# Two batches of a first layer open at once: other PSUM banks, other homes in SBUF, constants in two loads, new lists

## The chip, the cores and the metric

One NeuronCore of one Trainium2 chip runs the whole program. Its engines are called here as in the profile: PE (TensorE), DVE (VectorE), ACT (ScalarE), POOL (GpSimd) and SP (SyncE, which only issues transfers). The metric is the device time of one execution in microseconds (us), lower is better.

## The reference

Two layers follow each other for 8 batches of 256 tokens with 256 features. The first is a graph attention with 16 heads and two directions, in which each of the 256 tokens looks at the first 20 only. The second is a transformer block with adaptive norm, rotary embedding, full attention over 256 tokens (16 heads of 16) and a gated feed-forward part of width 1024.

```python
# first layer
row_zero = exp_v.sum(-1) == 0
q_exp = jnp.where(row_zero[..., None], 0.0, q[:, None, :])
self_feat = jnp.concatenate([exp_v, q_exp], axis=-1) @ W_self.T + b_self
for d in range(2):
    A = (adj_f if d == 0 else jnp.swapaxes(adj_f, 1, 2))[:, :, :20, :]
    cond, vb = A.sum(-1), A @ w_bias + b_bias
    # qh from self_feat, kh from its first 20 rows
    aff = jnp.where(mask, qh_kh / sqrt(dh), NEG) + vb      # mask: cond > 0
    output = output + out_projection(softmax(aff) @ kv)
x = exp_v + relu(output)
# second layer
nx = ada_rmsnorm(x, time_emb, ...);  q, k = rope(nx @ wq + bq), rope(nx @ wk + bk)
x = x + softmax(q k^T / sqrt(16)) v @ wo + bo
x = x + (gelu(nz @ w_gate) * (nz @ w_up)) @ w_down         # nz = ada_rmsnorm(x, ...)
```

## The kernel before

**Stages.** Each engine works through a list of steps written out by hand, `step(n)(b)` for part n of batch b, in that order and without skipping; semaphores join the engines. Lists of neighbouring batches are interleaved: the first layer of batch b + 2 stands beside the second layer of batch b. All big products are made of three float32r products of high and low halves (`product`, L2109), so that each operand is split by a copy on ACT (`...h`, `whigh`) and a subtraction on POOL or DVE (`...l`, `low` L597, `wlow` L592 on POOL and L1496 on DVE).

**First layer of a batch, front.** DVE sums the rows of x (`rowsum`, L1532), POOL marks zero rows (`nonzero`), SP stores that mask to memory and reads it back broadcast (`nz_store` L278, `nz_load` L283), POOL makes of it and of the condition column the start of the self features (`nzq`, L616). PE adds the self product (`selfm`), DVE joins them (`selfc`, L1538 and L1539), PE makes small key and value products (`small` L2179, `kT`), DVE spreads them (`kev`, `vb`, `kb`), PE makes `q0` and the affinity (`affm`, L2212). DVE counts the adjacency (`adjm`, L1522 to L1526), POOL makes mask and bias of it (`mask`).

**Back.** DVE multiplies by the mask (`am`, L1569), POOL adds the bias (`aadd`, L641) and subtracts the maximum (`asub`, L649), ACT takes the exponential, POOL normalises (`aprob`, L662), PE transposes the probabilities (`pTt`, L2228; copies `pTa` on ACT, `pTc` on DVE), PE multiplies with the values (`y`, L2240), DVE adds (`yadd`, L1598), PE transposes (`x1T`, L2152), DVE makes x1 (`x1add`, L1604).

**PSUM and SBUF.** Front and back of this layer share PSUM banks 3 and 4: `BANK = {"c": 0, "self": 3, "k0": 4, "v0": 3, "q0": (3, 4), "aff": 3, "pT": (4, 3), "y": 4, "x1": 3, ...}`. They share the buffer `l0` as well (q0T, kblk and kk of the front, pT and yT of the back), `self32` and `vblk`. So `selfm(0)` of batch b waits for `x1_ok` of batch b - 1, `nzq` and `small` for its `y_ok`. Banks 0 and 1 serve the condition products at the start (`cond_1`, `cond_2`) and then the scores.

**Second layer.** `nxT`, `qk`, `v`, the rotation (`rot` on DVE L1625, `radd` on POOL L690), `qkT`, `qkadd` (DVE, L1641 and L1642), `qklow` (POOL, L698), out to memory and back in stacked form (`high_out`, `low_out`, `q_stack`, `k_stack` on SP), then 16 score products `s` (L2302) with 16 maxima `mx` on DVE (L1650), their transpose `nmT` (L2311), a row copied by `nrows`, 16 products `st` (L2326) with 16 exponentials `exph` on ACT (L1047), `pv`, `oT`, `aT`, `wo`, then gate, up and down products.

**Loads at the start.** SP loads x, weights in pieces of 256 KB into eight slots (a piece waits for the `wlow` of the one before it in its slot) and constants in seven loads: `get_consts`, `get_wb`, the condition column (in `cond`), `get_vec`, `get_angles`, `get_rope`, `get_bo`. The condition table `tab` is made by DVE in `table` out of `cond_2`.

Of the kernel before, what the change touches and what calls it, by code (L numbers as in the profile page):

```python
# [9 lines left out]
ALU = mybir.AluOpType  # L10
# [15 lines left out]
KC = D // P  # L26
# [8 lines left out]
BEHIND = 2  # L35

# [8 lines left out]
K_ID, K_M8, K_M4, K_ONES, K_BK, K_ALL = 0, 128, 136, 140, 156, 284  # L45
# [19 lines left out]
def build(nc, x, xT, adj, condT, wall, wsmall, wcond, cols, rows_in, tabs, consts_in, out):  # L65
    ctx = ExitStack()
    with ctx:
# [3 lines left out]
        def sig(name, per=1):  # L71
# [42 lines left out]
        pT = l0[:, :].rearrange("p (d g s) -> p d g s", d=2, g=4)  # L114
        yT = l0[:, 0:512].rearrange("p (k s) -> p k s", k=KC)
# [34 lines left out]

        wcq, wc1, wc2 = vv[:].rearrange("p c n -> p (c n)")[:, 0:512], t1[:].rearrange("p c n -> p (c n)"), ya[:, :]
# [62 lines left out]
        BANK = {"c": 0, "self": 3, "k0": 4, "v0": 3, "q0": (3, 4), "aff": 3, "pT": (4, 3), "y": 4, "x1": 3,  # L214
# [27 lines left out]
        def _(sp):  # L242
# [117 lines left out]
            get_wb()  # L360
            load_x(1)
            nz_store(0)
            weights("self", 0)()
            cond()
            load_adj(0)
            nz_load(0)
            nz_store(1)
            get_vec()
            get_wsk()
            get_wsv()  # L370
            weights("q0", 1)()
# [2850 lines left out]
```

## Time and profile before

| what | us |
|---|---|
| median of 3 runs | 514.03 |
| lowest, highest | 509.83, 514.95 |
| the profiled execution | 512.82 |
| its span, first to last instruction | 511.0 |
| mean granted clock of TensorE | 0.960 of full |

The span is read from the trace of one execution; the runs are timed from outside. Busy times are sums over an engine's instructions, and the chain is followed back from the last instruction to whatever released each.

### The profile page before, as it was taken

The numbers are of one execution on the slowest core, as the hardware profiler recorded it, in microseconds if no ns is written. First come the engines' busy times: TensorE is split into PE (matmuls) and PEld (weight loads), VectorE is DVE, ScalarE is ACT, GpSimd is POOL, SyncE is SP. The second block draws the span as 40 slices with busy tenths as digits, with TensorE's granted clock in tenths as the row PEclk, the third lists the DMA queues.
The fourth block names the chain that finished last, engine by engine and source line by source line (L and its number), as shares of the span: only waits on it lengthen the run. The fifth ranks groups of instructions, "written<-read, shape, count | busy, mean of one in ns | idle before, by whom it ended". The sixth has DMA issues, their size and how long they took to land.

```text
span 511.0 us, 9893 instructions
## 1 busy us (share of the span) xinstructions
PE 450.1 (88%) x3728; PEld 391.5 (77%) x3728; DVE 321.6 (63%) x529; ACT 245.0 (48%) x472; POOL 270.3 (53%) x266
## 2 busy tenths in 40 slices
PE   0776766878899999989999998999899979999997
PEld 0674655757588789878979897889788957897896
DVE  1757666898689547936995597478834870840421
ACT  1144412434722884177436843675466328347431
POOL 4555588597745655654554583546831371132232
PEclk9985787999889999999999998999999999999999
DMA  6920264614320430053014401540032003210000
GB/s 177 339 112 3 96 109 158 182 32 155 106 52 3 127 104 22 22 175 101 22 58 106 135 2 44 106 149 0 4 119 89 3 18 129 63 45 2 21 22 22
DMA packets 35231, 41.30 MB, mean 81 GB/s; under 512 B 5872, under 2 KB 27888, under 8 KB 35056
## 3 DMA queue, kind: packets, MB, share of 16 engines
q1 hardware_dynamic: 35184, 40.67, 27.3%
q8 instruction: 30, 0.49, 0.4%
q14 instruction: 17, 0.14, 0.1%
HBM read 29.90 MB, written 10.49 MB: 79 GB/s over the span
## 4 chain that ended last, share of the span: by engine, by line
PE 67%; DVE 12%; POOL 9%; issue 5%; DMA 4%; ACT 2%; SPq 1%; DVEq 0%; POOLq 0%; ACTq 0%
PE ps L2109 33%; PE ps L2326 7%; PE ps L2341 6%; PE ps L2302 5%; PE ps L2152 4%; PE ps L2228 3%; PE ps L2212 3%; PE ps L2240 3%; PE ps L2179 2%; DVE nm L1650 2%; POOL aff L641 2%; POOL prob L662 2%; DMA vec<-cols 1%; PE ps L2353 1%; DVE aff L1569 1%
## 5 line engine op out<-in xcount | busy, mean ns | idle before, releaser
L1650 DVE TENSOR_REDUCE nm<-ps 128x2 f32<-128x512 f32 x128 | 83.9, 683 | 26.3 <-PE ps L2302 25.8
L2109 PE MATMUL ps<-splz,wh 128*128 128x256 f32 x512 | 96.3, 286 | 3.0 <-DVE ya L1642 1.8
L1047 ACT ACTIVATE ex<-ps 128x512 f32<-128x512 f32 x128 | 70.0, 598 | 35.4 <-PE ps L2326 33.7
L2109 PEld LDWEIGHTS ps<-splz,wh 128*128 128x128 f32 x512 | 79.3, 191 | 5.5 <-issue 4.7
L597 POOL TENSOR_TENSOR hs<-g,hs 128x512 fp32r<-128x512 f32 x32 | 42.0, 1316 | 72.3 <-ACT hs L1091 72.3
L2109 PE MATMUL ps<-splz,wl 128*128 128x256 f32 x256 | 72.3, 282 | 0.0
L2302 PE MATMUL ps<-kst,qst 96*128 96x256 f32 x256 | 51.6, 305 | 4.9 <-DVE nm L1650 4.0
L2109 PE MATMUL ps<-wh,hs 128*128 128x256 f32 x256 | 52.8, 286 | 0.7 <-POOL hs L597 0.7
L2326 PE MATMUL ps<-qst,kst 100*128 100x256 f32 x256 | 49.2, 303 | 2.7 <-DMA qst<-ex 2.5
L1694 DVE TENSOR_TENSOR g<-ps,g 128x512 f32<-128x512 f32 x32 | 22.0, 687 | 46.4 <-PE ps L2109 41.0
L2109 PEld LDWEIGHTS ps<-splz,wl 128*128 128x128 f32 x256 | 48.8, 191 | 0.0
L2326 PEld LDWEIGHTS ps<-qst,kst 100*128 100x128 f32 x256 | 36.1, 189 | 15.9 <-ACT ex L1047 10.5
L2302 PEld LDWEIGHTS ps<-kst,qst 96*128 96x128 f32 x256 | 38.1, 192 | 12.5 <-DVE nm L1650 9.4
L2109 PEld LDWEIGHTS ps<-wh,hs 128*128 128x128 f32 x256 | 42.5, 191 | 1.0 <-POOL hs L597 0.9
L2109 PE MATMUL ps<-splx,wh 128*128 128x256 f32 x192 | 39.1, 302 | 3.1 <-DVE res L1604 2.3
L641 POOL TENSOR_TENSOR aff<-aff,off 128x640 f32<-128x640 f32 x16 | 26.6, 1663 | 23.3 <-DVE aff L1569 23.3
L2109 PE MATMUL ps<-wh,sply 128*128 128x512 f32 (+1 forms) x128 | 37.5, 357 | 0.1
L2109 PE MATMUL ps<-wl,hs 128*128 128x256 f32 x128 | 36.2, 283 | 0.0
L1081 ACT ACTIVATE g<-ps 128x512 f32<-128x512 f32 x32 | 19.1, 597 | 35.1 <-PE ps L2109 34.5
L2109 PEld LDWEIGHTS ps<-splx,wh 128*128 128x128 f32 x192 | 32.0, 205 | 4.8 <-DVE res L1604 3.1
L2341 PE MATMUL ps<-ex,vv 128*32 128x256 f32 x512 | 35.1, 393 | 0.2 <-ACT ex L1047 0.2
L597 POOL TENSOR_TENSOR splz<-ya,splz 128x512 fp32r<-128x512 f32 x16 | 20.5, 1283 | 26.8 <-DVE ya L1674 21.3
(131 smaller groups left out, 997.1 us busy)
## 6 DMA issues: line engine op xcount, KB each, us to landing
qk_d<-ya SPq DMA_DIRECT2D x32, 256.0 KB, 3.9
qst<-qk_d SPq DMA_DIRECT2D x48, 128.0 KB, 2.5
kst<-qk_d SPq DMA_DIRECT2D x96, 64.0 KB, 2.4
ex<-wall SPq DMA_DIRECT2D x15, 256.0 KB, 6.8
aff<-adj SPq DMA_DIRECT2D x8, 440.0 KB, 3.9
res<-x SPq DMA_DIRECT2D x8, 256.0 KB, 2.7
xTs<-xT SPq DMA_DIRECT2D x8, 256.0 KB, 3.6
result<-res SPq DMA_DIRECT2D x8, 256.0 KB, 2.0
```

The lines of the kernel that those rows point to most:

```text
L597: pool.tensor_tensor(into, whole, high.bitcast(FP32), ALU.subtract).then_inc(signal.sem, 1)
L641: pool.tensor_tensor(aff[:, c], aff[:, c], off[:, :, c, :].unsqueeze(2).broadcast_to([P, 2, H, M]), ALU.add).then_inc(aa_ok.sem, 1)
L1047: act.activation(ex[:, h % EXR], ps[:, h % 2].rearrange("p (c s) -> p c s", c=TC), ACT.Exp, scale=SCALE).then_inc(ex_ok.sem, 1)
L1081: act.activation(g32[:, j % 2], ps[:, BANK["g"]].rearrange("p (k s) -> p k s", k=2), ACT.Gelu).then_inc(gelu_ok.sem, 1)
L1650: dve.tensor_reduce(nm[:, :, h % 2, h // 2], ps[:, h % 2].rearrange("p (c s) -> p c s", c=TC), AX.X, ALU.max, negate=True).then_inc(mx_ok. ...
L1694: dve.tensor_tensor(g, ps[:, BANK["u"]].rearrange("p (k s) -> p k s", k=2), g, ALU.mult).then_inc(hm_ok.sem, 1)
L2109: ins = pe.matmul(dst, lhs(a, k), rhs(c, k), start=first_ and n == 0 and m == 0, stop=last_ and n == len(ks) - 1 and m == 2, **kw)
L2152: ins = pe.transpose(dst[:, i * S + j * P:i * S + (j + 1) * P], src(i, j), ident)
L2212: ins = pe.matmul(ps[:, 3 + d, k * 8 * M:(k + 1) * 8 * M], q0T[:, d, k, c * P:(c + 1) * P], kblk[:, 2 * d + k].rearrange("p h m -> p (h m) ...
L2302: ins = pe.matmul(ps[:, bk, c * S:(c + 1) * S], qst[0:96, h // 2, c * P:(c + 1) * P], kst[0:96, h, :], start=True, stop=True)
L2326: ins = pe.matmul(ps[:, bk, c * S:(c + 1) * S], kst[0:100, h, c * P:(c + 1) * P], qst[0:100, h // 2, :], start=True, stop=True)
L2341: ins = pe.matmul(ps[32 * j:32 * j + 32, 2, (g % 2) * S:(g % 2 + 1) * S], vv[:, c, h * VW:h * VW + 32], ex[:, h % EXR, c, :], start=c == 0 ...
```

## The change

- PSUM: for batches 0 and 1 (`OPEN = 2`) the back of the first layer uses banks 0 and 1 instead of 4 and 3.
- SBUF: for these two, pT and yT lie in `ya` instead of `l0`; self features and value blocks of batch 1 lie in `g32`.
- Waits: `selfm(0)` of batches 1 and 2 waits for `am_ok` of the batch before instead of `x1_ok`; `nzq`, `small` and `vb` of batches 1 and 2 don't wait for the back of the batch before (batch 2 for that of batch 0). New waits: `pTt` of batch 0 on the first half of the table, of batch 1 on `x1_ok` of batch 0; `nzq(1)` on the rotated bias; the first `gelu` on `y_ok` of batch 1; `qkadd` of batch 0 and `s(0)`, `s(1)` of batch 0 on `x1_ps` or `x1_ok` of batch 1.
- Loads: column constants, condition column and label row come inside `consts` (now 348 columns), rope and bo in one load `late`; angles stay alone. Four loads fewer.
- All five lists are new, over the whole program.

The core of the diff, in this order: banks and homes, the wait of `selfm`, that of `pTt`, that of `qkadd` for batch 0:

```diff
-        BANK = {"c": 0, "self": 3, "k0": 4, "v0": 3, "q0": (3, 4), "aff": 3, "pT": (4, 3), "y": 4, "x1": 3,
+        BANK = {"c": 0, "self": 3, "k0": 4, "v0": 3, "q0": (3, 4), "aff": 3,
...
+        early = ya[:, :]
+        spare = g32[:].rearrange("p j i s -> p (j i s)")
+        selves = [self32[:], spare[:, 0:KC * S].rearrange("p (k s) -> p k s", k=KC)]
+        vblks = [vblk[:], spare[:, KC * S:KC * S + 512].rearrange("p (d g n) -> p d g n", d=2, g=4)]
+        def pT_of(b):
+            return (early if b < OPEN else l0[:, :]).rearrange("p (d g s) -> p d g s", d=2, g=4)
+        def back(b, n):
+            return (0, 1)[n] if b < OPEN else (3, 4)[n]
...
 -                        before(pe, x1_ok, b - 1)
+                        if b <= OPEN:
+                            before(pe, am_ok, b - 1)
+                        else:
+                            pe.wait_ge(x1_ok.sem, x1_ok.at(b - 1))
...
 -                    if n < 2:
+                    if n < 2 and b == 0:
+                        pe.wait_ge(tab_ok.sem, tab_ok.at(0, 4))
+                    elif n < 2 and b < OPEN:
+                        pe.wait_ge(x1_ok.sem, x1_ok.at(b - 1))
+                    elif n < 2:
                         pe.wait_ge(am_ok.sem, am_ok.at(b))
...
 -                        dve.wait_ge(c2_ps.sem, c2_ps.at(0))
+                        dve.wait_ge(x1_ps.sem, x1_ps.at(OPEN - 1))
```

The lists up to the first score product, before and after (k(0) for step k of batch 0, several parts together):

```
PE before:  cond_q selfm(0) small(0) kT(0) q0(0) affm0(0) cond_1 affm1(0) cond_2 pTt(0) y(0) x1T(0)
            selfm(1) small(1) nxT(0) kT(1) q0(1) affm(1) qk0,v0,qk1,v1(0) pTt(1) qkT(0) y(1) x1T(1)
            selfm(2) nxT(1) small(2) q0,kT(2) s(0)
PE after:   cond_q selfm(0) small(0) kT(0) q0(0) affm0(0) cond_1 affm1(0) selfm(1) cond_2 small1(1)
            pTt0,1(0) small0(1) kT(1) pTt2,3(0) q0(1) y(0) x1T(0) affm(1) nxT(0) qk0(0) pTt0,1(1) qk1(0)
            pTt2,3(1) selfm0(2) y(1) selfm1(2) x1T(1) qkT(0) v(0) small(2) kT(2) q0(2) nxT(1) affm0(2) s(0)
DVE before: ... am0 amax0 am1 ones0 amax1 asums0 asums1(0) table pTc(0) ones1 wlow-v yadd(0) wlow-qk0
            x1add(0) rowsum(2) selfc kev vb kb adjm(1) nxc(0) am0(1) wlow-qk1 am1(1) wlow-u0 amax(1)
            rot0(0) asums(1) rot1(0) pTc1(1) rowsum(3) pTc3(1) qkadd(0) yadd x1add(1) adjm selfc(2) ...
DVE after:  ... am0 amax0 am1(0) rowsum(2) amax1 asums0(0) selfc(1) table asums1 pTc1(0) kev vb kb(1)
            pTc3(0) ones1 adjm(1) yadd x1add(0) am0(1) wlow-v am1 amax0(1) nxc(0) amax1(1) wlow-qk0,qk1
            asums(1) wlow-u0 rowsum(3) rot0(0) pTc1,3(1) rot1(0) wlow-u1 yadd(1) selfc(2) qkadd(0)
            x1add(1) kev vb kb adjm(2) nxc(1) wlow-u2 am0(2) mx0(0) ...
POOL after: nonzero(0) fills xl(0) nzq(0) zeros0 vfill selfl(0) nonzero(1) mask(0) xl(1) aadd0 asub0
            aadd1(0) nzq(1) asub1 aprob(0) selfl(1) wlow-g0,g1,g2 nonzero(2) wlow-g3 mask(1) wlow-d0
            pow1(0) aadd0,1 asub0(1) nxl(0) asub1 aprob0(1) xl(2) aprob1(1) radd0(0) nzq(2) nonzero(3)
            radd1(0) zeros1 selfl(2) qklow(0) pow1(1) ...
SP after:   x(0) consts adj(0) w-self angles xT(0) nz_store(0) wcond-q w-q0 nz_load(0) wsv wsk w-q0b x(1)
            late xT(1) w-g2 wc1 w-qk0 nz_store(1) wc2 nz_load(1) x(2) w-v w-g0 w-g1 w-qk1 adj(1) w-g3
            xT(2) w-d0 x(3) w-d1 nz_store(2) w-u0 w-u2 w-u1 xT(3) nz_load(2) w-d2 w-d3 adj(2) high_out ...
```

## Rows read from the trace of the kernel before

**Rows 1.** The page: busy us of each engine; shares of the chain.

```profile
PE 450.1 (88%) x3728; PEld 391.5 (77%) x3728; DVE 321.6 (63%) x529; ACT 245.0 (48%) x472; POOL 270.3 (53%) x266
...
PE 67%; DVE 12%; POOL 9%; issue 5%; DMA 4%; ACT 2%; SPq 1%; DVEq 0%; POOLq 0%; ACTq 0%
```

**Rows 2.** Busy time by stretch: us, engines' busy us, clock, DMA share, GB/s.

```profile
0.00:94.60 94.60, 58.37 (x396) 49.79 (x397) 57.91 (x94) 29.93 (x61) 58.65 (x63) 0.84 0.50 145
94.60:118.10 23.50, 18.90 (x130) 15.60 (x129) 21.51 (x36) 8.30 (x17) 18.07 (x17) 1.00 0.30 78
...
160.00:400.00 240.00, 233.16 (x2057) 206.93 (x2057) 162.73 (x268) 137.06 (x256) 131.90 (x128) 0.99 0.26 74
```

**Rows 3.** The chain in order of time, to 140 us: start us, us, what.

```profile
4.23 4.42 DMA nz_d<-nz
...
17.04 1.12 POOL self L616 x2
...
41.69 1.29 POOL prob L662
...
50.77 0.70 DVE res L1604
...
64.90 0.84 DVE aff L1569
...
84.42 1.05 POOL ya L698
...
94.75 0.47 PE ps L2302 x4
```

**Rows 4.** DMA issues up to 60 us: count, KB each, median us to landing.

```profile
ex<-wall SPq DMA_DIRECT2D x10, 256.0 KB, 8.4
...
ya<-wcond SPq DMA_DIRECT2D x1, 1024.0 KB, 10.6
...
nzb<-nz_d SPq DMA_DIRECT2D x2, 128.0 KB, 7.7
...
const_sb<-consts SPq DMA_DIRECT2D x1, 142.0 KB, 3.7
...
vec<-cols SPq DMA_DIRECT2D x1, 18.0 KB, 7.3
```

**Rows 5.** DVE in order of time: start us, us, operation.

```profile
41.26 1.74 DVE L1513 TENSOR_SCALAR tab<-tab,vec 128x8 f32<-128x8 f32 x4
...
59.35 1.06 DVE L1522 TENSOR_REDUCE aff<-aff 128x80 f32<-128x880 int32 x1
```

**Rows 6.** PE in order of time: start us, us, operation, idle before.

```profile
32.80 4.76 PE L2144 MATMUL ps<-hT,ya 128*128 128x8 f32 x32 [1.07 <-ACT hT L952]
...
45.88 3.41 PE L2240 MATMUL ps<-l,vblk 128*64 128x256 f32 x16 [0.83 <-issue]
...
78.93 1.94 PE L2228 MATMUL ps<-const_sb,prob 128*128 128x128 f32 x8 [1.56 <-POOL prob L662]
80.66 1.92 PE L2152 MATMUL ps<-const_sb,t 128*128 128x128 f32 x8
...
111.25 1.06 PE L2228 MATMUL ps<-const_sb,prob 128*128 128x128 f32 x8
...
113.16 1.95 PE L2240 MATMUL ps<-l,vblk 128*64 128x256 f32 x16 [0.26 <-issue]
```

**Rows 7.** POOL in order of time.

```profile
33.50 2.52 POOL L641 TENSOR_TENSOR aff<-aff,off 128x640 f32<-128x640 f32 x1
...
65.99 1.99 POOL L641 TENSOR_TENSOR aff<-aff,off 128x640 f32<-128x640 f32 x1
...
99.88 1.54 POOL L641 TENSOR_TENSOR aff<-aff,off 128x640 f32<-128x640 f32 x1 [3.77 <-DVE aff L1569]
```

**Rows 8.** SP's queue in order of time.

```profile
86.12 2.42 SPq L308 DMA_DIRECT2D qst<-qk_d  x3
```

**Rows 9.** Busy time from 40 to 50 us, columns as in rows 2.

```profile
40.00:50.00 10.00, 6.89 (x32) 4.63 (x30) 7.81 (x19) 3.82 (x8) 4.67 (x3) 0.56 0.00 0
```

More of the change, by code:

```diff
@@ L62, in at, with build @@
         return value
-def build(nc, x, xT, adj, condT, wall, wsmall, wcond, cols, rows_in, tabs, consts_in, out):
+def build(nc, x, xT, adj, wall, wsmall, wcond, late_arr, tabs, consts_in, out):
     ctx = ExitStack()
@@ L357, in _ @@
+            nz_store(0)
+            cond()
             weights("q0", 0)()
-            load_xT(0)
-            get_consts()
-            get_wb()
+            nz_load(0)
+            get_wsv()
+            get_wsk()
+            weights("q0", 1)()
             load_x(1)
[L362 to L366, printed above, removed]
-            nz_store(1)
[L368 to L371, printed above, removed]
@@ L733, in _ @@
             aadd(1)(0)
+            nzq(1)
             asub(1)(0)
@@ L736, in _ @@
             aprob(1)(0)
-            xl(1)
+            selfl(1)
             wlow("g", 0)()
-            nzq(1)
-            pow1(0)
-            selfl(1)
-            wlow("d", 0)()
             wlow("g", 1)()
@@ L745, in _ @@
             nonzero(2)
+            wlow("g", 3)()
             mask(1)
-            nxl(0)
+            wlow("d", 0)()
+            pow1(0)
             aadd(0)(1)
@@ L750, in _ @@
             asub(0)(1)
+            nxl(0)
             asub(1)(1)
             aprob(0)(1)
+            xl(2)
+            aprob(1)(1)
             radd(0)(0)
-            aprob(1)(1)
+            nzq(2)
+            nonzero(3)
             radd(1)(0)
-            vfill()
-            xl(2)
+            zeros(1)()
+            selfl(2)
             qklow(0)(0)
             qklow(1)(0)
-            wlow("o", 0)()
-            nzq(2)
             pow1(1)
-            wlow("g", 3)()
-            selfl(2)
+            wlow("d", 1)()
             mask(2)
+            aadd(0)(2)
             nxl(1)
-            aadd(0)(2)
+            wlow("d", 2)()
             aadd(1)(2)
@@ L790, in _ @@
             asub(1)(3)
-            nonzero(4)
             aprob(0)(3)
+            nxl(2)
+            aprob(1)(3)
+            radd(0)(2)
             xl(4)
-            aprob(1)(3)
             alow(0)
-            nxl(2)
+            x1bias(0)
             nzq(4)
+            radd(1)(2)
             pow2(0)
-            radd(0)(2)
-            radd(1)(2)
             selfl(4)
@@ L1702, in _ @@
             rowsum(0)
-            rowsum(1)
+            ones(0)()
             wlow("self", 0)()
@@ L1716, in _ @@
             am(1)(0)
-            ones(0)()
+            rowsum(2)
             amax(1)(0)
             asums(0)(0)
+            selfc(1)
+            table()
             asums(1)(0)
-            table()
             pTc(1)(0)
-            pTc(3)(0)
-            ones(1)()
-            wlow("v", 0)()
-            yadd(0)
-            wlow("qk", 0)()
-            x1add(0)
-            rowsum(2)
-            selfc(1)
             kev(1)
@@ L2171, in step @@
                 def step(b):
-                    if which == 0:
-                        before(pe, y_ok, b - 1)
+                    if which == 0 and b > OPEN:
+                        pe.wait_ge(y_ok.sem, y_ok.at(b - 1))
                     pe.wait_ge(self_ok.sem, self_ok.at(b))
@@ L2764, in _ @@
             st(3)(3)
-            up(2, 0)(2)
-            x1T(5)
+            selfm(0)(6)
+            selfm(1)(6)
             st(4)(3)
@@ L2771, in _ @@
             st(7)(3)
-            selfm(0)(6)
-            selfm(1)(6)
+            small(1)(6)
+            small(0)(6)
             st(8)(3)
@@ L3148, in _ @@
             down(3, 1)(7)
-_IN = ["x", "xT", "adj", "condT", "wall", "wsmall", "wcond", "cols", "rows_in", "tabs", "consts"]
+_IN = ["x", "xT", "adj", "wall", "wsmall", "wcond", "late", "tabs", "consts"]
 def kernel(**inputs):
```

1310 lines of the change are left out of this document (660 added, 650 removed).

## The prediction, made before the changed kernel ran

> **What bounds the kernel now.** I read the page's busy shares and its chain first, then the busy time by stretch, then the chain in order of time over the first 120 us, and last each engine's queue in order of time. TensorE (PE) is busy 88% of the span and carries 67% of the chain [rows 1]. That mean hides two regimes [rows 2]. From 160 to 400 us PE is busy 233.2 of 240 us, so nothing is won there unless PE has less to do, and this change leaves its matmuls as they are. Up to 94.6 us, where the first score product s(0) of batch 0 starts, PE is busy only 58.4 of 94.6 us, DVE and POOL some 58 us each, and the mean granted clock is 0.84. There a serial chain decides. Whatever brings s(0) of batch 0 forward with the same work behind it shifts the rest of the program by the same amount, since the rest is mostly bound by PE. The chain's stations are in [rows 3]: nzq (17.04), batch 0's second probability (41.69), x1 (50.77), batch 1's first masked affinity (64.90), the last low half (84.42 to 85.5), s(0) (94.6; 94.75 in the chain).
>
> The work of the first layer in the chain lies twice in a row. Batch 1's self product can't start before batch 0's x1 (it ends at 51.5), because both halves of the layer use PSUM banks 3 and 4, and the 13.4 us from 51.5 to 64.9 are its front alone: self product, self sum, small products, q0, affinity.
>
> **The change, step by step.**
>
> *1. The start.* Batch 0's chain waits for the column constants, which took 7.3 us to land [rows 4]: POOL's nzq(0) starts at 17.04, when vec is there [rows 3]. Now all constants come in the second load. What is left to wait for is the nonzero mask's way through memory and the condition product. The mask's store is issued at 4.23 as before (x, rowsum and nonzero stand as early) and takes 4.42 us [rows 3]. In front of it now lie 1.6 MB (x, constants, adj, self, angles, xT), which at 300 to 370 GB/s have passed by about 7; I put its landing at 9 to 9.5. The two reloads of the window took 7.7 us in the median with 0.7 MB and more ahead of them, a load on a nearly free queue 3.7 (consts) [rows 4]; now two weight loads are ahead, so about 4. That is nzq(0) at 13.5, 3.5 us earlier (bounds: 0 if the reload takes 7.7, 4 if it takes 3.7).
>
> Four loads fewer are issued; only vec stood on the path. The rows show loads overlapped in one queue: the 18 KB of vec took 7.3 us, those of 256 KB of wall 8.4 [rows 4]. So the saving is where vec ended a wait, and no more. The Trainium skill, "DMA: Bandwidth & Descriptors" (Anatomy of one DMA and Rules for kernel authors), puts about 2 us of fixed cost on each DMA and advises to coalesce small ones; four of them end to end would give 8 us by it, an estimate, and a time near 500; the trace's overlap speaks against it.
>
> *2. Batch 1's front is put between batch 0's back.* On batch 0's own path this costs. DVE now runs selfc(1) (1.3 us) and the table (2.9 us, its last four operations 1.74, [rows 5]) before asums(1) of batch 0, and the table waits for cond_2 (4.8 us on PE, [rows 6]), itself now behind selfm(1) (2.3 us). By my walk: selfm(1) 29.2 to 31.7, cond_2 to 35.5, table to 38.4, asums(1) to 39.7, second probability at 39.8 instead of 41.69. Of the 3.5 us, 1.9 are left. Then DVE has kev, vb, kb of batch 1 (1.9), ones (1.2) and adjm(1) (three operations like the 1.06 us one, 3.2, [rows 5]) ahead of yadd(0), and PE has q0 of batch 1 (3.5) ahead of y(0). x1(0) comes out at 51.7 instead of 50.77: 1 us lost. SP holds nz_store(1) until rowsum(1), about 21, and the 1 MB of wc2 is queued behind it. At the 10.6 us that this load took [rows 4] it lands at 32, when cond_2 wants it.
>
> *3. What it buys.* When x1T(0) ends, batch 1's q0 and its table of masks are done. affm(0)(1) needs only the engine, and its masked product follows at about 52.5, not at 64.90: 12.4 us won. This is the whole gain.
>
> *4. What is given back.* Before, 15.8 us passed from that product to the first transpose behind it in the list, qkT(0) at 80.66 [rows 6]. Now y(1) and x1T(1) stand ahead of qkT(0), and qkadd waits for x1_ps of batch 1. From the same rows: POOL's pow1, two aadd (1.54, [rows 7]), two asub (1.27), nxl (1.27), aprob, xl(2), aprob: last probability at 65.5; transposes to 67.5; pTc; y (1.95 to 3.41, [rows 6]) beside selfm(2) (1.4 each half); yadd 0.7; x1T 0.7; qkT at 72.2. That is 19.7 us against 15.8, 3.9 lost. On DVE wlow u1, yadd and selfc(2) (2.6 us) lie in the same stretch; they are hidden behind y(1) while radd(1) of batch 0 is out at 70.6. DVE's first qkadd is at 73, the last low half at 76.8 (before 85.5). zeros(1) (1.8) and selfl(2) (1.3) on POOL stand ahead of it, but end at 74, when its input comes. Gain here: 8.7.
>
> *5. From there to s(0).* SP issues the stacks from 86.12 on without a wait, 0.8 us each [rows 8], and s(0) starts 9.1 us behind the last low half. Nothing in that stretch changes for the first half of the heads; weights d2 and d3 are now loaded before. kb(2), affm(0)(2) and am(0)(2) have to come before s(0); by my walk they end at 84. So s(0) at 76.8 + 9.1 = 85.9, 8.7 us earlier.
>
> *6. Behind it.* From 94.6 to 118.1 DVE is busy 21.5 of 23.5 us [rows 2], so the 16 maxima stay bound by DVE. Two splits (2 x 0.64) have moved ahead of them, one PE half of v has moved behind. I take 0.3 (bounds +1.3 and -0.8). The lists of batches 2 to 7 are new throughout. PE is idle 6.8 us from 160 to 400 [rows 2], and reordering can take some of it or add to it. No row tells which; I take 0, with 3 us either way, about half of that idle time.
>
> The walk leaves two things out. DVE splits stretch POOL's operations: aadd took 1.99 us beside wlow and 2.52 beside the cast of ones, 1.54 alone [rows 7]. That is 0.4 to 1.0 per collision, and before had nearly the same ones in its chain, so I charge 1 us. Against it stands 1 us for a TensorE clock that falls less; the two cancel. The page "SBUF — State Buffer" of the Trainium skill (Who interferes with whom) says that DVE's operations with two SBUF inputs, and its casts, take a port pair exclusively, and the other engine fully blocks. By that, five splits (3.4), one cast (1.5) and the adj product (1.1) would cost POOL up to 6.0 us, and the result would be 510. The trace agrees in kind, with at most 1.0 us of the cast's 1.67 lost.
>
> Sum: 12.4 at batch 1's masked product (in it are the 3.5 of the start and the 4.5 lost up to x1), less 3.9 in step 4 makes 8.5 at qkT; the smaller steps up to the low half add 0.2, the maxima 0.3: 9 us. The profiled execution took 512.82 us (span 511.0), so it becomes 503.8 with a span of 502. The median of the runs shown, 514.03, is 1.2 above the profiled one; I put the median at **504.5 us**.
>
> **The rivals.**
>
> *A, less comes through (508 to 513).* Round trips on SP's queue. load_x(3) waits for POOL's wlow d0; u0 waits for DVE's wlow qk0; wlow u0 stands on DVE ahead of rot(0)(0). After qk0 at 59 the way over SP, DMA, ACT and back took 4.7 us by my walk with a free queue. Of it 2.7 were the landing. A load of wall took 8.4 us in a loaded one [rows 4]: rot comes 5.7 us later and the gain falls to 3.3, that is 510. For it: SP's list is served in order, and four loads stand behind the same split. Against: only some 0.8 MB are in the queue then. The port rule above would end here too (510); 0.05 of A's chance is its.
>
> *B, the clock comes on top (496 to 500).* The granted clock falls to 0.56 from 40 to 50 us [rows 9], a stretch in which PE waits in small gaps. Groups of probability transposes take up to 1.94 us there against 1.06 at the higher level, y 3.41 against 1.95 [rows 6]. Four groups and one y would give 3.5 + 1.5 = 5 us at most: 499.5. For it: batch 1's q0 and self product fill gaps on PE behind POOL's probabilities. Against: POOL and DVE decide most stations, and time won on PE there is lost again in their queues.
>
> *C, slower (516 to 519).* The overlap fails in time while the new order holds: y(1) and x1T(1) ahead of qkT(0) and the qkadd wait. If am(0)(1) came no earlier than 64.9, the 3.9 us of step 4 would be pure loss: 517. Turning point: am(0)(1) at 61. To be that late, the table or batch 0's back would have to slip 8.5 us more than in my walk, as by a late wc2 (landing after 40). The largest landing in the rows is 10.6 us, so I see little for it.
>
> *D, nothing that can be measured (512 to 515):* 9 us won at s(0), then given back by new waits in batches 1 to 3. That PE is 97% busy behind 160 us [rows 2] speaks against more than 3 us of it.
>
> **How the numbers follow.** The measurement tells about 1% from no change. Forecast (gain 6 to 12.5) 0.45; B 0.20; A 0.20; D 0.08; C 0.07. Faster by over 1% is below 508.9: the forecast, B, and a third of A, 0.72. Slower by over 1% is above 519.2: the tail of C, 0.05. Same: 0.23. The range runs from B's fast side without its last bit, 497, to the border of A and D, 512, and leaves about 2 in 10 out.
>
> **What would show it.** In the profile of the changed kernel: nzq(0) at 13 to 14, no wait for vec (step 1). Second probability of batch 0 at about 40, x1 at about 51.7: if x1 comes at 46, my step 2 overcharges. am(0)(1) within 1.5 us behind x1(0) (step 3). Last low half at 74 to 80 and s(0) of batch 0 at 83 to 89 (steps 4, 5). DVE waiting on ACT's wh ahead of rot means A. Transposes of probabilities at 1.1 to 1.3 us and a clock of 0.95 in 30 to 90 mean B. PE busy in 160 to 400 below 0.95 would show that the later lists are worse, and would make the prediction wrong even with steps 1 to 5 right.

## The result and the profile after

| what | before, us | after, us |
|---|---|---|
| median (20 runs each, side by side) | 510.98 | 504.53 |
| lowest, highest | 506.23, 514.95 | 502.31, 510.40 |
| ratio to before | 1 | 0.9885, 95% interval 0.9856 to 0.9914 |
| profiled execution, span | 512.82, 511.0 | 506.42, 504.6 |
| mean granted clock of it | 0.960 | 0.963 |

The change makes the kernel 1.15% faster. The medians are of all 20 runs, while the ratio here and in every later table leaves out runs more than 1.5% above the fastest of the same kernel (two of the 20 after, and of the experiments below e3's 521.66, for one). The median of 504.53 is what was forecast (504.5), but the sum behind it was too large: it had 9 us of gain on a kernel that took 514.03 in the three runs shown. As forecast, 504.5 on 514.03 is a ratio of 0.9815, which lies outside the measured interval. In the runs beside it the kernel before took 510.98, and the gain is 6.4 us, in the medians as in the spans.

The page after, its busy shares, its clock line and its chain (to set beside [rows 1]):

```profile
PE 447.5 (89%) x3728; PEld 387.9 (77%) x3728; DVE 322.7 (64%) x529; ACT 246.6 (49%) x474; POOL 270.0 (54%) x266
...
PEclk9788779889999999999998999999999999999999
...
PE 54%; DVE 15%; DMA 10%; POOL 8%; issue 6%; SPq 5%; ACT 2%; DVEq 0%; POOLq 0%; ACTq 0%
```

And the stretches that answer to [rows 2], up to the first score product s(0) of batch 0, from there to its first `st`, and behind 160 us:

```profile
0.00:88.30 88.30, 58.35 (x416) 50.36 (x416) 60.85 (x97) 32.91 (x68) 60.06 (x64) 0.85 0.54 158
88.30:113.90 25.60, 18.34 (x100) 14.52 (x101) 20.84 (x34) 4.49 (x9) 17.96 (x15) 0.87 0.25 42
160.00:400.00 240.00, 232.94 (x2044) 205.54 (x2044) 160.75 (x265) 139.05 (x256) 132.03 (x130) 0.99 0.26 75
```

PE does the same 58 us of work in front of s(0), in 88.3 us instead of 94.6. Behind 160 us it is busy 232.9 of 240, as before: the gain is made at the start and carried through. The chain of the kernel after, in order of time, with the stations of [rows 3] in it:

```profile
4.23 1.26 POOL nz L619
5.51 4.92 DMA nz_d<-nz
10.45 4.71 DMA nzb<-nz_d
15.26 1.12 POOL self L631 x2
...
21.20 4.80 PE ps L2124 x24
...
32.39 2.93 PE ps L2124 x12
35.32 3.73 PE ps L2160 x32
...
55.35 0.83 DVE aff L1584
...
69.49 1.28 POOL prob L677
70.80 1.27 POOL t L705
72.07 1.38 issue
73.52 1.56 POOL self L631 x2
75.28 1.24 POOL t L705
...
80.72 1.30 POOL ya L713
```

L2124 is the big products (24 matmuls of q0 of batch 0, then selfm(1) and (0) of batch 1), L2160 is `cond_2`, L1584 the masked product am(0)(1), L713 the last low half. The chain no longer holds a wait for vec, and no front of batch 1 stands between x1(0) (53.22) and am(0)(1) (55.35).

### The profile page after: what moved, and what is told of

Its sections match the earlier page's. It is cut to its first block, busy times and chain, and to the rows that moved or that the text cites. A ratio compares the mean times of both kernels' runs of the same rounds, so it can differ in the third digit from the quotient of the medians.

```text
span 504.6 us, 9889 instructions
## 1 busy us (share of the span) xinstructions
PE 447.5 (89%) x3728; PEld 387.9 (77%) x3728; DVE 322.7 (64%) x529; ACT 246.6 (49%) x474; POOL 270.0 (54%) x266
## 4 chain that ended last, share of the span: by engine, by line
PE 54%; DVE 15%; DMA 10%; POOL 8%; issue 6%; SPq 5%; ACT 2%; DVEq 0%; POOLq 0%; ACTq 0%
PE ps L2124 27%; PE ps L2349 6%; PE ps L2364 5%; PE ps L2325 4%; DMA nz_d<-nz 3%; PE ps L2231 3%; DMA nzb<-nz_d 3%; DVE nm L1665 2%; PE ps L2168 2%; PE ps L2251 2%; DMA kst<-qk_d 2%; SPq L342 2%; SPq L354 2%; PE ps L2263 2%; POOL t L705 2%
## 5 line engine op out<-in xcount | busy, mean ns | idle before, releaser
L2124 PE MATMUL ps<-splz,wh 128*128 128x256 f32 x512 | 96.3, 286 | 0.4 <-issue 0.4
L1062 ACT ACTIVATE ex<-ps 128x512 f32<-128x512 f32 x128 | 70.6, 597 | 44.8 <-PE ps L2349 43.5
L2124 PEld LDWEIGHTS ps<-splz,wh 128*128 128x128 f32 x512 | 78.5, 189 | 3.0 <-issue 2.2
L2124 PE MATMUL ps<-splz,wl 128*128 128x256 f32 x256 | 71.9, 281 | 0.0
L2124 PE MATMUL ps<-wh,hs 128*128 128x256 f32 x256 | 51.9, 285 | 1.1 <-POOL hs L610 1.0
L2124 PEld LDWEIGHTS ps<-splz,wl 128*128 128x128 f32 x256 | 48.3, 189 | 0.0
L2124 PE MATMUL ps<-wh,sply 128*128 128x256 f32 (+1 forms) x128 | 39.9, 370 | 6.3 <-DVE wl L1511 5.1
L2124 PEld LDWEIGHTS ps<-wh,hs 128*128 128x128 f32 x256 | 41.6, 188 | 1.8 <-POOL hs L610 1.7
L2124 PE MATMUL ps<-splx,wh 128*128 128x256 f32 x192 | 40.4, 309 | 2.5 <-DVE aff L1584 1.2
L2124 PEld LDWEIGHTS ps<-splx,wh 128*128 128x128 f32 x192 | 32.9, 211 | 4.5 <-DVE aff L1584 1.5
L2124 PE MATMUL ps<-wl,hs 128*128 128x256 f32 x128 | 35.8, 280 | 0.0
L2124 PEld LDWEIGHTS ps<-wh,sply 128*128 128x128 f32 x128 | 24.7, 203 | 10.6 <-DVE wl L1511 5.5
L677 POOL TENSOR_TENSOR prob<-aff,arc 128x640 f32<-128x640 f32 x16 | 20.4, 1273 | 19.5 <-PE ps L2251 12.4
```

What stands on the lines that cost most here:

```text
L677: pool.tensor_tensor(prob[:, :, 0:M], aff[:, c].rearrange("p d h m -> p (d h) m"), arc[:, c, :].unsqueeze(2).broadcast_to([P, 2 * H, M]), ...
L1062: act.activation(ex[:, h % EXR], ps[:, h % 2].rearrange("p (c s) -> p c s", c=TC), ACT.Exp, scale=SCALE).then_inc(ex_ok.sem, 1)
L2124: ins = pe.matmul(dst, lhs(a, k), rhs(c, k), start=first_ and n == 0 and m == 0, stop=last_ and n == len(ks) - 1 and m == 2, **kw)
```

## The experiments

All start times in us, read from one profiled execution each; the time is the median of the runs (4 to 20 of them). For e2 (530.93 us) and e8 (520.30) the profiled execution was the slowest of its kernel, so that their stations may lie some us late. The kernel before ran beside every group of kernels and its median moved from 510.98 (result) over 511.8 (e1 to e4), 512.5 (e5 to e8) and 513.7 (e9 to e11) to 514.8 (e12), so times of different groups are compared by the ratio. "Low half" is the start of POOL's two `qklow(0)` of 2.5 us together, "flags" the start of POOL's nzq(0).

| kernel | flags | x1(0) | am(0)(1) | low half | s(0) | time | ratio to before |
|---|---|---|---|---|---|---|---|
| before | 17.04 | 50.77 | 64.90 | 83.19 | 94.59 | 510.98 | 1 |
| after | 15.26 | 53.22 | 55.35 | 79.48 | 88.27 | 504.53 | 0.9885 |
| e1 | 15.18 | 51.48 | 63.76 | 81.39 | 92.77 | 509.10 | 0.9954 |
| e7 | 15.09 | 50.72 | 63.01 | 80.90 | 92.29 | 509.93 | 0.9940 |
| e2 | 15.74 | 53.78 | 80.22 | 104.45 | 113.11 | 525.75 | 1.0243 |
| e8 | 15.49 | 52.20 | 68.11 | 90.50 | 99.57 | 517.13 | 1.0080 |
| e3 | 14.34 | 49.76 | 50.85 | 74.58 | 83.37 | 503.74 | 0.9845 |
| e5 | 14.80 | 55.35 | 57.49 | 79.83 | 88.95 | 508.47 | 0.9896 |
| e6 | 15.60 | 56.48 | 58.62 | 81.02 | 90.42 | 508.86 | 0.9894 |
| e11 | 15.35 | 50.80 | 52.82 | 76.11 | 84.84 | 508.89 | 0.9896 |
| e4 | 14.79 | 54.16 | 56.29 | 78.42 | 87.23 | 506.38 | 0.9884 |
| e9 | 14.47 | 50.55 | 52.23 | 75.84 | 84.60 | 503.86 | 0.9808 |
| e10 | 14.99 | 51.39 | 53.38 | 76.81 | 85.77 | 502.29 | 0.9781 |
| e12 | 14.68 | 50.52 | 51.61 | 76.76 | 86.69 | 505.36 | 0.9854 |

**What the loads bring alone.** e1 is the kernel before with the constants in two loads; banks, homes and lists are left as they were.

```diff
-get_vec()  get_wb()  get_rope()  get_bo()     # SP's list
+get_late()                                    # vec, wb, cT are columns of consts
```

> The kernel before, with only the loads of the change: column constants, condition column and label row come inside the constants, rope and bo in one load where rope stood; every list is otherwise that of before, every wait for the front of the next batch stays. Theory (the overlap is the source of the gain, the loads give only the end of one wait): nzq(0), at 17.04 us before, starts when the reloaded mask is there, at 14 to 15; s(0) of batch 0 moves from 94.6 to about 92.5, st(0) from 118.1 to about 116; time 509 against 511, ratio 0.996. Rival (the start is what was won: in the changed kernel the gain of batch 0 at st(0) is only 4.2 us): s(0) at 90 or earlier, ratio 0.990 or less.

Measured: 0.9954 (0.9917 to 0.9991), flags at 15.18, s(0) 1.8 us earlier. The loads are worth 1.8 us at the flags, about as much at s(0), nearly a third of what the whole change brings there. That the two numbers agree is in part chance: between them x1(0) came 0.7 us later than before, since cond_2 took 6.92 us instead of 4.76 (32 matmuls, most of them at the lower clock), and batch 1's front ran faster than before (granted clock 1.00 from 52 to 60 us, 0.57 before). Of the 8 us that four loads end to end would have given, nothing more than these 1.8 was seen.

**What the overlap brings.** e2 and e8 are the kernel after with batch 1's front put back behind x1(0) on every engine.

```diff
 # PE's list, e8
-selfm(0..1)(1) ahead of cond_2; small, kT, q0 of (1) ahead of y(0)
+selfm(0..1)(1), small, kT, q0 of (1) behind x1T(0), then nxT(0)
 # POOL's list
+pow1(0), selfl(1), mask(1) behind wlow("g", 3)
```

> The changed kernel with one part undone: the self product of batch 1 waits again for x1 of batch 0, and the steps of batch 1's front (selfm, small, kT, q0 on PE; selfc, kev, vb, kb, adjm on DVE; selfl on POOL; selfb and q0c on ACT) stand behind x1 of batch 0. Banks, homes, loads and all other steps stay as changed. Theory (the overlap is the whole gain): x1(0), at 53.2 in the changed kernel, comes 3 to 6 us earlier since nothing stands before it, but am(0)(1) goes from 55.35 back to about 62, the last low half of batch 0 from 82.0 to about 89, and the time from 504.5 to 511 or 515, ratio to the kernel before 1.00 to 1.01. Rival (loads and new lists bring the gain, the overlap only reshuffles): ratio stays at 0.99.

In e2 am(0)(1) came only at 80.22, 26 us behind x1(0), and the ratio was 1.0243 (1.0149 to 1.0336). Most of that was my own placement. I had nxT(0) ahead of q0(1) on PE; it waits for POOL's pow1(0), and that stood behind mask(1), which waits for the adjacency on DVE. So I did it again without that knot.

> The kernel after with the overlap undone, like e2_front_behind_x1, but with pow1(0) ahead of selfl(1) and mask(1) on POOL and nxT(0) behind q0(1) on PE, so that q0(1) no longer stands behind both. Theory, the overlap is the gain: x1(0) at 53 to 54, am(0)(1) 14 to 16 us behind it as in the kernel before (68 to 70, 55.4 in the kernel after, 80.2 in e2), s(0) 101 to 103, ratio 1.010 to 1.025. Rival 1, the overlap brings little, and e2 lost its time to the place of nxT(0) alone: am(0)(1) by 60, s(0) by 93, ratio below 1.0. Rival 2, what cost e2 its time is not nxT(0) but the tail of the front itself: am(0)(1) later than 76, ratio 1.02 or more.

```profile
52.20 0.69 DVE L1619 SCALAR_TENSOR_TENSOR res<-ps,res 128x512 f32<-128x512 f32 x1 [1.21 <-PE ps L2168]
...
68.11 0.82 DVE L1584 TENSOR_TENSOR aff<-ps,msk 128x640 f32<-128x640 f32 x1 [3.50 <-PE ps L2233]
```

These are x1(0) and am(0)(1) of e8: 15.9 us apart again (14.1 before, 2.1 after). am(0)(1) is 12.8 us later than in the kernel after, s(0) 11.3; the ratio is 1.0080 (1.0047 to 1.0113) against 0.9885, two points or 10 us. So the overlap is worth about 10 us in the time (11 to 13 at the stations of one profile that was 3 us above e8's median), and the new order without it is slower than the kernel before. That is rival C's mechanism, shown by itself. Rival 1 (the overlap brings little) is out.

**Where the rest went: casts and memsets, or the clock?** In the kernel after, DVE's cast `ones(0)` stands second in its list. POOL's 2-element `nonzero` beside it (after, then before, then e5, where the cast is moved away):

```profile
4.23 1.25 POOL L619 TENSOR_SCALAR nz<-rs 128x2 f32<-128x2 f32 x1 [3.81 <-DVE rs L1547]
```

```profile
3.97 0.23 POOL L606 TENSOR_SCALAR nz<-rs 128x2 f32<-128x2 f32 x1 [3.54 <-DVE rs L1532]
```

```profile
4.25 0.23 POOL L619 TENSOR_SCALAR nz<-rs 128x2 f32<-128x2 f32 x1 [3.82 <-DVE rs L1547]
```

Beside the cast `nonzero` takes 1.0 us longer, at the head of the chain. So e3 moved it, and the two memsets ahead of POOL's selfl(0), which I held to stretch DVE's `bout` (a small operation, on 128x2).

```diff
 # DVE's list
-rowsum(0)  ones(0)()  wlow("self", 0)() ...
+... rotated_bias()  ones(0)()  am(0)(0) ...
 # POOL's list
-nzq(0)  zeros(0)()  vfill()  selfl(0)
+nzq(0)  selfl(0)  zeros(0)()  vfill()
```

> The changed kernel with two steps moved: the cast ones(0) on DVE from the second place of its list behind rotated_bias, and on POOL zeros(0) and vfill (memsets) from ahead of selfl(0) to behind it. Theory (a cast on DVE and POOL's work exclude each other: nonzero took 1.25 us beside the cast against 0.23, and bout on DVE 1.67 us beside the memset against 0.15): the mask's store is issued at 4.3 instead of 5.51, nzq(0) starts at 14.0 instead of 15.26, bout takes 0.2, q0 of batch 0 starts at 19 instead of 21.2, and s(0) of batch 0 at about 86.5 instead of 88.3; time 1 to 2 us below the changed kernel. Rival (these lie beside the chain; loads of weights decide the start, as q0's second piece lands at 18.4): nzq(0) moves, q0 and s(0) don't.

e3 brought 4.9 us at s(0), far more than expected. If the moved steps had earned that, each half alone should bring its part:

> The kernel after, with VectorE's cast ones(0) behind rotated_bias and nothing else moved (POOL's two memsets stay ahead of selfl(0)). Theory, the cast holds POOL up: the first nonzero takes 0.23 us again instead of 1.25, the flags are stored 0.9 us earlier, nzq(0) starts at 14.4 (15.26 in the kernel after), and everything behind it is earlier by that, unless the chain is set by the memsets: x1(0) between 49.8 and 52.4, s(0) between 83.4 and 87.4, ratio to the kernel before 0.978 to 0.987. Rival, the 0.9 us are lost again at once in the wait for the q0 high part (wh, 18.39): prob and x1(0) as in the kernel after (42.5 and 53.2), s(0) 88.3.

> The kernel after, with POOL's two memsets behind selfl(0), and the cast ones(0) left in second place. Theory, they hold VectorE up: nonzero keeps its 1.25, nzq(0) stays at 15.3, bout takes 1.2 or less instead of 1.67, selfl(0) ends 1.7 us earlier (18.2 for 19.8), and x1(0) comes 0.5 to 1.5 us earlier than the 53.2 of the kernel after; s(0) 86.8 to 87.8. If the memsets carry the most of what the two moves brought together, s(0) is at 85 or less. Rival, no effect: s(0) 88.3.

Both theories fell. Each half alone had x1(0) later (55.35 and 56.48, against 53.22), and neither ratio, 0.9896 and 0.9894, is below that of the kernel after. In e5 even the flags came 0.5 us earlier, and batch 0's first probability 1.1. What differs is `cond_2` and the table behind it. e5, then e3; PE's cond_2, DVE's first table operation, 32 small matmuls in both:

```profile
34.10 6.83 PE L2160 MATMUL ps<-hT,ya 128*128 128x8 f32 x32
...
41.04 0.23 DVE L1523 TENSOR_SCALAR tab<-ps,const_sb 128x8 f32<-128x8 f32 x1 [4.07 <-PE ps L2160]
```

```profile
31.31 4.10 PE L2160 MATMUL ps<-hT,ya 128*128 128x8 f32 x32
...
35.83 0.22 DVE L1523 TENSOR_SCALAR tab<-ps,const_sb 128x8 f32<-128x8 f32 x1
```

The granted clock from 32 to 42 us is 0.50 in e5, and 1.00 in e3 up to 34. The same instructions take 2.7 us longer, selfm of batch 1 in front of them 1.2 (2.9 against 1.7), and everything on batch 0's path waits for the table. So the theory became: x1(0) hangs on where TensorE's clock falls between 25 and 45 us, and moving a cast only shifts that.

**The clock, tried directly.** e9 is e5, and e10 the kernel after, each with 30 transposes of the identity added in four places where PE waits anyway. They write to bank 6, which nobody has used yet; nothing reads them.

```diff
+def keep_clock(n):
+    for i in range(n):
+        pe.transpose(ps[:, 6, (i % 4) * P:(i % 4 + 1) * P], ident, ident)
 # PE's list
+keep_clock(10)   # ahead of small(1)(0)
+keep_clock(6)    # ahead of kT(0)
+keep_clock(6)    # ahead of affm(0)(0)
+keep_clock(8)    # ahead of selfm(0)(1)
```

> e5_cast_moved_alone with 30 transposes of the identity added to PE's list, into a PSUM bank that nobody reads yet, in four places where PE waits anyway: 10 ahead of small(1)(0), 6 ahead of kT(0), 6 ahead of affm(0)(0), 8 ahead of selfm(0)(1). In e5 the granted clock was 0.50 to 0.64 from 30 to 44 us: cond_2 took 6.83 us, the table started at 41.04, x1(0) at 55.35. Theory, the clock in 30 to 44 is what sets x1(0), and it fell because PE had been idle in those gaps: with the gaps filled the clock stays at 1.0 up to 35 us or longer, selfm(0 and 1)(1) and cond_2 take 1.6 and 4.1 us (2.7 and 6.8 in e5), the table starts by 37, x1(0) at 50 to 51, s(0) at 83.5 to 85 (88.95), time 503 to 505 (508.5). Rival, the clock doesn't follow these gaps, or the added work costs more than it brings: clock near 0.5 in 32 to 42 as in e5, x1(0) at 55 to 56, time 508 to 509.

> The kernel after with the same 30 added transposes. There the granted clock was 0.50 from 19 to 25 us, 0.57 from 32 to 36, 0.50 from 40 to 42; x1(0) at 53.22. Theory: q0(0) in 20 to 26 runs at the full clock (0.28 us instead of 0.41 for a matmul, 1.5 us saved), prob(0) second at 39.5 to 41, x1(0) at 50 to 52, s(0) 85 to 87, time 1.5 to 3 us less than the 504.5 of the kernel after. Rival, no gain: the clock falls elsewhere instead, x1(0) 53 or later, time 504.5 or more.

Both came out as the theory had it. Busy time and clock from 30 to 44 us, columns as in [rows 2], first of e5 and then of e9:

```profile
30.00:44.00 14.00, 12.43 (x69) 11.63 (x68) 7.83 (x22) 6.73 (x14) 6.39 (x6) 0.52 0.36 105
```

```profile
30.00:44.00 14.00, 12.01 (x111) 10.60 (x110) 10.55 (x27) 6.88 (x13) 10.08 (x10) 0.86 0.47 141
```

The clock goes from 0.52 to 0.86, PE gets 111 instructions through instead of 69 (6 of them are added transposes), x1(0) comes 4.8 us earlier, s(0) 4.3, and the ratio falls from 0.9896 (0.9851 to 0.9941) to 0.9808 (0.9765 to 0.9850). The kernel after gains 2.5 us at s(0) and 3.3 in the span, and comes to 502.29, ratio 0.9781 (0.9731 to 0.9831), the best of all that ran. The interval of e10 lies clear of that of the kernel after, the interval of e9 just clear of that of e5; these are four runs each. In detail the clock did not do all that was foreseen: in e9 it fell to 0.50 from 28 to 30 us and was back at 31, and affm(1)(0) took 2.50 us. Which idle piece brings it down is not settled; that filling them helps is.

The clock column doesn't show all of it. From 20 to 24 us it reads 1.00 in e5 and in e10, yet the same matmuls of q0(0) come at different paces there, first e5, then e10:

```profile
22.46 0.63 PE L2124 MATMUL ps<-splx,wh 128*128 128x256 f32 x2
```

```profile
22.43 0.40 PE L2124 MATMUL ps<-splx,wh 128*128 128x256 f32 x2
```

All 24 take 4.6 us in e5 and 3.1 in e10, behind the added transposes. So part of what these bring lies where the column shows no difference, and why is open; the duration of one matmul has to be read beside the clock.

e11 put e3 and e4 together, and its two theories were exactly these two readings.

> The kernel after with both the edits of e3_casts_and_memsets_moved and of e4_two_orders. Theory A, they add up as far as e4 brought anything: x1(0) as in e3 (49.8), s(0) 82.5 to 83.4, time 503 to 504, ratio 0.980 to 0.986. Theory B, what e3 gained at x1(0) came from where the clock fell and not from the moved work, so that another small edit upsets it: x1(0) at 53 or later, s(0) 87 or later, time 505 to 508. e5 and e6, each with one half of e3's edit, had x1(0) at 55.4 and 56.5, which speaks for B.

The median, 508.89, lies just above theory B's range and far from A's: with e3's edits in full it is as slow as e5 and e6. Its profiled execution had the good pattern (x1(0) at 50.80, as A had it). It took 505.82, and its eight executions run from 502.73 at a mean clock of 0.973 to 510.59. So one kernel meets more than one pattern, and the profile shows one of them. Whether e3's moves are better than the kernel after in the mean stays open: e3's interval, 0.9757 to 0.9932, holds the ratios of the kernel after and of e11 too.

**The given-back part.** e4 moves splits and transfers in the stretch behind am(0)(1).

```diff
 # DVE's list
+wlow("qk", 0) behind am(0)(1), wlow("qk", 1) behind am(1)(1), wlow("v", 0) behind asums(1)(1)
 # SP's list
+nz_load(2) right behind nz_store(2), weights("u", 2) behind load_xT(3)
```

> The changed kernel with two orders altered in the stretch in which batch 1's back and batch 0's q, k lie: DVE's splits of qk stand directly behind am(0)(1) and am(1)(1), that of v behind asums(1)(1), with the load of u2 behind xT(3); and SP's nz_load(2) stands directly behind nz_store(2). Theory (that stretch took 26.7 us from am(0)(1) to the last low half instead of the forecast 24.3, because qk(0)(0) waited until 64.7 for the splits and POOL's nzq(2) until 73.5 for the reload): qk(0)(0) starts at 62 to 63, nzq(2) doesn't wait, the last low half is out at 80 instead of 82.0, s(0) at 86.5 instead of 88.3, time 1 to 2 us below the changed kernel. Rival (POOL's own work in that stretch is the bound, 20 us of operations in a row): the waits move to the next step, the last low half stays within 0.5 us of 82.

From am(0)(1) to the low half it takes 22.1 us, where the kernel after takes 24.1. But x1(0) is 0.9 us later, s(0) only 1.0 earlier, and by batch 2 nothing is left: 0.9884 (0.9820 to 0.9948), the same as after. The rival was nearer.

e12 adds 38 more transposes to e10: 6 behind `cond_2`, 12 ahead of x1T(0), 20 ahead of qk(0)(0).

> e10_after_with_filling_transposes with 38 further transposes of the identity: 6 behind cond_2, 12 between y(0) and x1T(0) (PE waits 2.35 us there), 20 between nxT(0) and qk(0)(0) (5.1 us). In e10 the clock is 0.50 from 36 to 41 and from 52 to 58; there affm(1)(1) takes 2.50 us instead of 1.35 and the first qk(0)(0) runs at half the clock. Theory, what it brought up to 42 us it brings here too: affm(0)(1) and affm(1)(1) take 1.35 each, am(0)(1) at 52 to 52.7 (53.38 in e10), the second one 2 us earlier (54.8 for 56.8), the clock in 60 to 70 above 0.9 (0.66), s(0) at 83.5 to 84.8 (85.77), time 0.5 to 2 us under e10's 502.3, ratio 0.974 to 0.979. Rival, the chain from am(1)(1) on is not PE's, and the added work only stands in the way: s(0) 85.5 to 87, time 502.5 to 504.

The first half came true: am(0)(1) at 51.61, am(1)(1) at 53.88 (56.80 in e10), a clock of 1.00 from 44 to 90 us. The time did not follow: the ratio is 0.9854 (0.9800 to 0.9908), no better than e10. Why the low half came no earlier than in e10 (76.76 against 76.81), POOL of e12:

```profile
66.75 1.27 POOL L705 TENSOR_TENSOR t<-t,xr 128x512 f32<-128x512 f32 x1 [0.73 <-DVE xr L1643]
71.24 1.12 POOL L631 TENSOR_SCALAR self<-nzb,qc,const_sb 128x256 f32<-128x256 f32 x2 [3.22 <-DMA nzb<-nz_d]
72.33 0.24 POOL L619 TENSOR_SCALAR nz<-rs 128x2 f32<-128x2 f32 x1
72.53 1.26 POOL L705 TENSOR_TENSOR t<-t,xr 128x512 f32<-128x512 f32 x1
```

nzq(2) stands in POOL's list between the two `radd` of batch 0 and waits 3.22 us for the flags of batch 2 (1.45 in the kernel after, 0.45 in e10). Their reload was issued 2.1 us earlier than in e10 (64.83 against 66.91), but took 6.3 us to land instead of 3.6. All that was gained at am(1)(1) is waited off there, and the second radd, on which qkT and the low halves hang, comes at 72.53, in e10 at 72.20. This is not the whole loss. At s(0) e12 is 0.9 us behind e10, at batch 3's first `st` 1.6, at batch 4's 4.2, and 2.9 at the end; what happens between batches 3 and 4, far behind the added work, was not looked into.

**The cast put in elsewhere.** e7 is e1 with `ones(0)` second on DVE.

> The kernel before with the merged constants (so e1_loads_only), and the cast ones(0) moved to the second place of VectorE's list, as in the kernel after: the suspected cost by itself, put into a kernel that does not have it. Theory: nonzero(0) takes 1.2 us instead of 0.23, the flags are stored about 1 us later, nzq(0) starts at 16.2 (15.18 without), x1(0) and s(0) are 1 us later (52.5 and 93.8), ratio 0.9955 to 1.000. Rival, the reload of the flags is paced by something else: nzq(0) within 0.3 of 15.18 and s(0) within 0.5 of 92.8.

The test missed its object. In this list the constants land later, so that the cast began at 6.39 and not beside `nonzero`, which kept its 0.23; the flags stayed at 15.09. What it did meet was POOL's memset: the cast took 2.72 us instead of 1.22. The time is that of e1 within the error.

## Why the prediction was right, and where only by luck

**Step 1, the start: right in kind, half in size.** No wait for vec is left, as forecast. The flags came at 15.26 and not at 13.5, so 1.8 us were won and not 3.5. The store went out at 5.51 where the forecast had 4.23: 1.0 us is the cast on `nonzero`, 0.3 that x landed later. It took 4.92 us, which the forecast's landing at 9 to 9.5 allowed for, and the reload 4.71 instead of about 4. I had read the cast's price on an aadd from [rows 7] and had not looked at what stands beside the cast at its new place. Moving it (e5) gave `nonzero` its 0.23 back, but the flags came only 0.5 us earlier.

**Step 2, batch 0's own path: what was missed is `bout`, held up on DVE, and the clock.** selfm of batch 1 started at 32.39 where I had 29.2. Of the 3.2 us, 1.8 come from step 1. From the flags to am(1)(0), which selfm waits for, it took 1.2 us more than before (16.26 against 15.07): 0.5 is q0 of batch 0, whose 24 matmuls took 4.80 us in the chain and 4.31 before, and 0.7 its later start, since kT stood behind `bout` on DVE. The rest is rounding in my walk. At the higher pace q0 could have been had in 3.1 (e10). cond_2 was charged with 4.8 us in the text, but my walk went on from 31.7 to 35.5, with 3.8: a slip that did no harm, since it took 3.9, the clock being up again. The second probability came at 42.48 where I had 39.8, x1(0) at 53.22 instead of 51.7. The forecast let 1 us of clock cancel against 1 us of port collisions. Both were small numbers where x1(0) lay between 49.76 and 56.48 in the profiles of kernels that differ in the place of one to three steps.

**Step 3, the overlap: right, in mechanism and in place.** am(0)(1) follows x1(0) by 2.1 us (x1T and affm(0) ran at the lower clock). It is 9.55 us earlier than before, not 12.4. Of the missing 2.85, 1.5 are those of x1(0), and 1.3 lie between the two (0.8 in my walk). e8 gives the price of the overlap alone: 12.8 us at am(0)(1). "This is the whole gain" holds but for step 5 and the loads.

**Step 4, what is given back: right in kind, 2.4 us too small.** From am(0)(1) to the end of the last low half 26.7 us passed, 24.3 in my walk and 20.6 before. So 6.1 are given back, not the 3.7 of the same two stations in the forecast. The term that was left out is nzq(2). It waits 1.45 and takes 1.56 us ahead of radd(1)(0), which ended at 76.5 instead of some 73.5 (70.6 in my walk, moved by the 2.85 of before). The reload was late since SP's list had it behind load_xT(3), which waits until POOL has read the old xT in xl(2). SP's queue and POOL in the kernel after:

```profile
68.45 0.33 SPq L289 DMA_DIRECT2D xTs<-xT  x1
68.88 0.38 SPq L302 DMA_DIRECT2D nzb<-nz_d  x1
```

```profile
67.08 1.30 POOL L610 TENSOR_TENSOR splx<-xTs,splx 128x512 fp32r<-128x512 f32 x1
...
73.52 1.56 POOL L631 TENSOR_SCALAR self<-nzb,qc,const_sb 128x256 f32<-128x256 f32 x2 [1.45 <-DMA nzb<-nz_d]
```

The three pieces of u ahead of it, which wait for DVE's splits, were out by 65.0. This is rival A's mechanism, a transfer held up in SP's order by another engine, but with another transfer and another engine than I had named. In e4 the reload went out at 60.79 instead of 68.88, nzq(2) waited for nothing, and 2.0 of these 6.1 us came back; e12 shows the same wait as the wall once PE is quicker.

**Step 5, from the low half to s(0): wrong, in our favour.** "Nothing in that stretch changes" was false. It took 9.1 us before and takes 6.3. Every kernel with the old lists has 8.9 to 9.2 (e1, e7), every one with the new ones 6.1 to 7.4, without the overlap too (e8: 6.6). Before, both low halves were written ahead of all stacks; now a stack goes out between the two writes. SP's issues before, then in the kernel after:

```profile
85.71 0.36 SPq L298 DMA_DIRECT2D qk_d<-ya  x1
...
86.63 1.43 SPq L308 DMA_DIRECT2D qst<-qk_d  x1
...
88.63 2.72 SPq L323 DMA_DIRECT2D kst<-qk_d  x6
```

```profile
82.03 0.38 SPq L317 DMA_DIRECT2D qk_d<-ya  x1
82.45 0.97 SPq L327 DMA_DIRECT2D qst<-qk_d  x2
83.52 2.73 SPq L342 DMA_DIRECT2D kst<-qk_d  x6
```

So the last piece that the first heads need was issued 4.2 us behind the low half, and 5.9 before. My 0.8 us for each stack was a wrong reading of [rows 8]: the 2.42 us are of three issues, the second took 1.43 and the others 0.4 to 0.5. Of the 1.6 us won, about 0.5 is the stack moved ahead and about 1.0 that no issue took 1.43 here. Why one does is open; in e12 one does again (7.4 us). PE's list, which had q0 of batch 2 ahead of s(0), now has s(0) wait for the transfer alone. So 3.5 us of gain at the low half became 6.3 at s(0), where 8.7 stood in the forecast.

**Step 6, behind it: the forecast of nothing held on the whole.** The first `st` of batch 0 gained 4.2 us (2.1 less than s(0), since the second half of the stacks took 5.67 us to land and s(8) waited). Batch 1's gained 6.5, batches 2 to 7 between 4.8 and 6.6, the end 6.4.

**The rivals.** A's delay in SP's order was there, with 2 to 3 us (nzq(2)) and not 5.7. B, the clock on top, did not come by itself; e10 shows that it was to be had, with 2.5 to 3.3 of the 5 us that B had put on it. C's mechanism is shown by e8: 4.6 us above the kernel before in the medians, where C had 3. The port rule of the Trainium skill ("SBUF — State Buffer", Who interferes with whom) was right on the cast (1.0 of its 1.2 us were lost on POOL, where [rows 7] had shown 1.0 of 1.67), and its 6.0 us in all did not appear: the gain was 6.4, not 3.

The sum, then: 9 forecast, less 2.85 up to am(0)(1) (start, clock), less 2.4 (batch 2's flags), plus 2.8 (stacks), less 0.2 behind them makes 6.4. The last line of the forecast held one more slip: 503.8 and 1.2 are 505.0, and I wrote 504.5. That the number came out exact is luck: the gain fell 3.1 us short of the 9.5 that lie between 514.03 and 504.5, and the kernel before was 3.1 us faster in the runs beside it than in the three shown. What was right is the mechanism, the place of the gain and its order of size.

## What to carry to other kernels

Price an overlap by its last shared wait, and then walk every queue behind it up to the next point where all meet: here some 12 us were bought (12.8 at am(0)(1) by e8) and 6 of them were handed over again, partly to a small transfer that had been early enough until then. Where PE waits in small gaps, read the granted clock of those stretches and the duration of one matmul in them before anything else, and try some harmless matmuls in the gaps before moving other work about; a kernel that seems better by the order of two steps may only have met another clock. Three runs of a kernel whose executions spread over 8 us gave its median 0.6% too high (514.03 against 510.98 in 20), half of what the change brings.

## What the runs showed of the hardware that I had not expected

- Transposes into an unused PSUM bank, put in places where PE idles, raised the granted clock of 30 to 44 us from 0.52 to 0.86 and took 0.9 points off the ratio (e9 against e5), 1.0 point in e10 against the kernel after. PE had been idle 2.7, 1.1, 0.9 and 1.2 us in these places and busy in between.
- Where the clock falls differs between the profiles of near twins: x1(0) at 49.76, 53.22, 55.35, 56.48 in four kernels which differ in the place of one cast and two memsets. How much of this is the edit is not shown, for it also differs between executions of one kernel: in e11, 502.73 at a mean clock of 0.973, 509.14 at 0.952.
- A clock column of 1.00 does not say that matmuls run at their best pace: two of them took 0.63 us in e5 and 0.40 in e10 at the same place of q0(0).
- An operation on 128x2 can take as long as what stands beside it on the other engine: POOL's 0.23 became 1.25 beside DVE's cast, and DVE's `bout`, 0.15 alone, 1.24 beside POOL's subtraction selfl(0) (e6). The 1.67 of the kernel after, which I had put down to the memsets, ended with the same subtraction (bout at 19.88, selfl(0) at 19.85) and began 0.4 us ahead of it, beside the last memset. A cast beside a memset took 2.72 instead of 1.22 (e7).
